# A transformer batch loop on one core: a deferred finish started later on VectorE, and unread products added on TensorE

## What is computed

```python
x = x + LN(attn1(LN(x)))      # 16 heads of 16, rotary, causal, window of 250
s = LN(x)                     # the second source
y = attn2(s)                  # full attention, keys and values through a 64-wide projection
x2 = rmsnorm(s + y) * n1w
out = x2 + shared(x2) + sum over the two chosen of 8 experts of gate * (swiglu(x2 @ W1) @ W2[e])
x = x + LN(rmsnorm(out) * n2w)
```

## Time and profile before

| | us |
|---|---|
| median of 3 runs | 2101.24 (2096.93 to 2102.88) |
| profiled execution, its own time | 2093.5 |
| its span, first to last instruction | 2091.7 |
| PE busy, DVE busy, ACT busy, POOL busy | 1893.1, 1370.5, 828.7, 381.4 |

### The profile page before, as it was taken

One profiled execution on the slowest core, in us unless ns is written; L12 is line 12 of the kernel. 1 busy time (PEld: TensorE's weight loads), 2 busy tenths in 40 slices (PEclk: granted clock), 3 DMA queues, 4 the chain that ended last, 5 costly groups with the idle time before them and its releaser, 6 DMA issues.

```text
span 2091.7 us, 28659 instructions
## 1 busy us (share of the span) xinstructions
PE 1893.1 (91%) x9484; PEld 1082.9 (52%) x9484; DVE 1370.5 (66%) x4293; ACT 828.7 (40%) x1730; POOL 381.4 (18%) x675
## 2 busy tenths in 40 slices
PE   6868898999999998999989999999989999899886
PEld 4343455636455464644646455553646546464565
DVE  6457464775858576585866857586675858668264
ACT  3534434254333534335442453326343353534310
POOL 1346013101221013200241012210122002410000
PEclk8676879999999997999999999899989999899898
DMA  2027102200141100401032010321014110220312
GB/s 84 2 81 277 46 32 92 101 25 28 42 152 42 42 31 27 177 12 52 22 112 101 2 51 32 122 80 42 11 42 152 42 49 24 100 103 2 131 51 100
DMA packets 33314, 141.95 MB, mean 68 GB/s; under 512 B 4368, under 2 KB 15248, under 8 KB 28560
## 3 DMA queue, kind: packets, MB, share of 16 engines
q1 hardware_dynamic: 29840, 121.27, 16.0%
q0 software_dynamic: 3328, 18.88, 2.4%
HBM read 118.11 MB, written 20.97 MB: 66 GB/s over the span
## 4 chain that ended last, share of the span: by engine, by line
PE 63%; DVE 27%; issue 6%; ACT 3%; POOL 0%; DMA 0%; SPq 0%; DVEq 0%; ACTq 0%; POOLq 0%
PE fb L820 12%; PE ot L767 11%; PE fb L797 8%; PE sm L725 8%; DVE negmax L1118 6%; PE st L753 4%; PE st L693 3%; DVE acc L1311 2%; DVE sm L1115 2%; PE st L709 2%; PE dn L693 2%; PE fb L816 2%; PE sm L753 2%; DVE stats L1032 2%; PE dn L735 1%
## 5 line engine op out<-in xcount | busy, mean ns | idle before, releaser
L611 ACT ACTIVATE probs<-st 128x512 f32<-128x512 f32 (+3 forms) x832 | 397.9, 507 | 452.9 <-PE st L753 450.1
L820 PE MATMUL fb<-w_r,h_r 128*128 128x512 f32 x1536 | 434.1, 415 | 0.0
L725 PE MATMUL sm<-k_t,q_t 48*128 48x512 f32 (+3 forms) x864 | 321.2, 457 | 65.1 <-DVE negmax L1115 39.0
L753 PE MATMUL st<-q_t,k_t 64*128 64x512 f32 (+3 forms) x832 | 307.4, 464 | 16.7 <-ACT probs L611 16.5
L820 PEld LDWEIGHTS fb<-w_r,h_r 128*128 128x128 f32 x1536 | 268.5, 189 | 103.7 <-issue 57.5
L1118 DVE TENSOR_REDUCE negmax<-sm 128x1 f32<-128x512 f32 x416 | 270.7, 685 | 78.2 <-PE sm L725 77.8
L725 PEld LDWEIGHTS sm<-k_t,q_t 48*128 48x128 f32 x864 | 146.6, 197 | 298.6 <-DVE negmax L1115 117.4
L1115 DVE CUSTOM_DVE_ANT_0 sm<-sm,mask_qk 128x384 f32<-128x384 f32 (+1 forms) x448 | 204.3, 465 | 111.9 <-PE sm L725 110.3
L797 PE MATMUL fb<-stack,wup_r 128*128 128x512 f32 x768 | 267.3, 468 | 3.2 <-DVE sg L1289 3.1
L767 PE MATMUL ot<-probs,v_s 128*32 128x512 f32 (+3 forms) x2048 | 266.0, 549 | 2.3 <-POOL probs L477 2.3
L436 POOL TENSOR_TENSOR stack<-rot,stack 128x256 fp32r<-128x256 f32 x64 | 50.0, 781 | 1000.2 <-ACT stack L547 1000.2
(11 more groups left out here) (173 smaller groups left out, 2511.0 us busy)
## 6 DMA issues: line engine op xcount, KB each, us to landing
w_r<-w_parts SPq DMA_DIRECT2D x32, 2048.0 KB, 7.9
wup_r<-wup_parts SPq DMA_DIRECT2D x64, 512.0 KB, 4.4
w_parts<-w_r POOLq DMA_DIRECT2D x4, 2048.0 KB, 9.3
x_s<-in_L_attn_query SPq DMA_DIRECT2D x8, 512.0 KB, 4.8
q_t<-rot_b SPq DMA_DIRECT2D x256, 4.0 KB
wup_parts<-h_r POOLq DMA_DIRECT2D x2, 2048.0 KB, 8.2
x_kept<-o_s SPq DMA_DIRECT2D x8, 512.0 KB, 3.0
h_s<-in_L_ffn_W_experts POOLq DMA_DIRECT2D x8, 512.0 KB, 5.7
```

The source lines that it names most:

```text
L611: nc.scalar.activation(probs[:, n % PSLOTS, 0:hi - lo], score_bank(m)[:, 0:hi - lo], ACT.Exp, scale=float(D) ** -0.5).then_inc(s_ex, 1)
L725: mm(max_bank(w, a)[:, 0:hi - lo], q_t[r:r + MROW, b, t * P:(t + 1) * P], k_t[r:r + MROW, b, lo:hi], start=True, stop=True).then_inc(s_sm, 1)
L753: mm(score_bank(w)[:, 0:hi - lo], k_t[r:r + SK, b, j * P:(j + 1) * P], q_t[r:r + SK, b, lo:hi], start=True, stop=True).then_inc(s_st, 1)
L820: last = mm(fb[q % 2][:, :], h_r[:, h, m, rows], w2_r[:, k % 2, w, m, :], start=(m == 0 and n == 0), stop=(m == NH - 1 and n == 2))
```

## The change

`unread(bank, n)` issues n products of the identity with a piece of the output weights into a bank; nobody reads them. In batch 1, which has no e, they stand where later batches multiply e's last sets: 6 behind the transposes of xa, 4 after tile 2 and 4 after the last stacks in `heads`, and 2 in each of the first four units of the attention. In batches 1 to 7, 2 more stand in the middle stage between the transposes of xn and the wait for their copies. On DVE the generators are taken apart: `gates(f)` is stepped as before, and `finish(e)` begins at m = 30, with two steps to a unit.

```diff
--- before.py
+++ after.py
@@ -67,6 +67,7 @@
 SOURCE_FIRST, SOURCE_STEPS = 18, 2
 STEPS_AT_LAST = 9
 SOURCE_FROM = 36
+FINISH_FROM, FINISH_STEPS = 30, 2
 
 
 LEAD_WIDE, TAIL_WIDE = (range(2 * GH, LEAD - GH), range(0, LEAD - GH)), ALL - LEAD + 4
@@ -840,6 +841,11 @@
                 if t == NT - 1:
                     last.then_inc(s_gl, 1)
 
+            def unread(bank, n):
+
+                for _ in range(n):
+                    mm(bank[:, 0:E], ident[:, :], wout_t[:, 0, :], start=True, stop=True)
+
             def in_pairs(w, wide):
 
                 return (() if w % 2 else (w, w + 1)) if wide else (w,)
@@ -849,8 +855,11 @@
                     if f is not None and a == 0:
                         if m == ROWS_FROM:
                             experts_rows(f, i)
-                        if e is not None and m in LAST_OUT_AT:
-                            expert_out(e, OUT_LEAD, LAST_OUT_AT.index(m))
+                        if m in LAST_OUT_AT:
+                            if e is not None:
+                                expert_out(e, OUT_LEAD, LAST_OUT_AT.index(m))
+                            else:
+                                unread(fb[1], 2)
                     if a == 0 and m == LAST_STACKS_AT:
                         if f is not None:
                             pe.wait_ge(s_xh, (f + 1) * N_XH)
@@ -907,12 +916,14 @@
                         last = project_rows(st[m][:, (t % 2) * E:(t % 2 + 1) * E], w, xn_t, t)
                     last.then_inc(s_pj, 1)
 
-            def heads(i, a, f):
+            def heads(i, a, f, second=False):
 
                 def beside(t):
                     if f is not None:
                         for q, m in OUT_HEADS[a][t]:
                             expert_out(f, q, m)
+                    elif second and a == 0:
+                        unread(fb[0], 2 * len(OUT_HEADS[a][t]))
 
                 for t in range(NT):
                     if t >= 2:
@@ -946,10 +957,12 @@
                 transpose_rows(xa, pair, s_tp)
                 if e is not None:
                     out_rows(e, OUT_ROWS)
+                elif f is not None:
+                    unread(fb[1], 6)
                 pe.wait_ge(s_tc, i * N_TC + NC)
                 if f is not None:
                     pe.wait_ge(s_pr, i * N_PR)
-                heads(i, 0, e)
+                heads(i, 0, e, f is not None)
                 if f is None:
                     pe.wait_ge(s_w, 16 * N_LOADS)
                 attention(i, f, e, 0)
@@ -957,12 +970,11 @@
                 if f is not None:
                     for q in OUT_FIRST:
                         out_rows(f, q)
-
-                    for _ in range(2):
-                        mm(dn[:, 0:E], ident[:, :], wout_t[:, 0, :], start=True, stop=True)
-
+                    unread(dn, 2)
                 pe.wait_ge(s_xn, i + 1)
                 transpose_rows(xn, pair, s_tp)
+                if f is not None:
+                    unread(st[1], 2)
                 pe.wait_ge(s_tc, i * N_TC + 3 * NC)
                 for c in range(NC):
                     last = mm(st[0][:, :], wc_s[:, c, :], xn_t[:, c, :], start=(c == 0), stop=(c == NC - 1))
@@ -1159,15 +1171,13 @@
                 beside(NT)
 
             def attention(i, f, e, a, more):
-                def beside():
-                    if f is not None and a == 0:
-                        yield from gates(f)
-                    if e is not None and a == 0:
-                        yield from finish(e)
-                    if a == 1 and more:
-                        yield from first_source(i + 1)
-
-                others, begin = beside(), (GATES_FROM, SOURCE_FROM)[a]
+                none = iter(())
+                if a == 0:
+                    others = gates(f) if f is not None else none
+                    later = finish(e) if e is not None else none
+                else:
+                    others, later = first_source(i + 1) if more else none, none
+                begin = (GATES_FROM, SOURCE_FROM)[a]
                 for m in range(-LEAD, ALL):
                     if a == 0 and m == LAST_STACKS_AT:
                         copy_stacks(i, a, NT - 1)
@@ -1191,7 +1201,13 @@
                                 expert_out(f, q)
                     if m >= begin:
                         next(others, None)
+                    if a == 0 and m == FINISH_FROM:
+                        run(others)
+                    if a == 0 and m >= FINISH_FROM:
+                        for _ in range(FINISH_STEPS):
+                            next(later, None)
                 run(others)
+                run(later)
                 normalise(i, a, NGR - 1)
                 out_now(f, sorted({q for part in OUT_END[a] for q, m in part}))
```

## The result

| | before | changed |
|---|---|---|
| median, us (6 runs each) | 2100.47 | 2109.04 (2103.36 to 2115.69) |
| ratio | | 1.0048 [1.003, 1.0066] |
| profiled execution, own time / span | 2093.5 / 2091.7 | 2103.36 / 2101.5 |
| mean granted clock | 0.926 | 0.924 |

A forecast was written before the change was run, and what follows sets the result against it. The prediction took TensorE (busy 91%) as the bound, losing time waiting for DVE and running at 1.2 GHz after such waits. Its terms, -6.7 - 5.7 + 2 = -10.4 us, took 2101.2 to 2090.8 us, range 2072 to 2108.

The forecast's parts named there:

- Part one: Batch 1's first stage: unread products keep the clock up, 50.8 us against 57.46, a gain of 6.7 us.
- Part two: Middle stage, batches 1 to 7: two products stop four clock falls, 6.4 us gained less 0.7 delay: 5.7 us.
- Part three: First attentions of batches 2 to 7: moved finish delays unit 38, 0.3 us more in each, 2 us lost.
- I leave batches 3 and 6 their extra falls: Part three's assumption that the first attentions of batches 3 and 6 (63.1 and 60.8 us) keep their additional clock falls.
- Rival (d): Units 16 to 22 of first attentions: four more batches fall like batch 3, +8 us, 2109 us; chance 0.16.
- (a): First attentions: the clock holds behind the last maxima too, -37 us, 2064 us; chance 0.10.
- (b): Middle stage: the two products do not hold the clock, -4 us, 2097 us; chance 0.14.
- (c): Batch 1's first stage: the clock falls despite the products, -2 us, 2099 us; chance 0.13.

The follow-up runs named there:

- e1: Kernel before plus all unread products of the change, finish stepped as before; 2106.11 us, ratio 1.0044.
- e12: Changed kernel with no finish step at units 35 to 37, three unread products at unit 38 and one at unit 22; 2081.50 us, ratio 0.9909.
- e14: Changed kernel with six unread products in the middle stage instead of two; 2105.05 us, ratio 1.0027.
- e3: Kernel before plus batch 1's unread products only; 2095.77 us, ratio 0.9989.
- e4: Kernel before plus only the two unread products in the middle stage of batches 1 to 7; 2117.03 us, ratio 1.0085.
- e6: e3 plus four unread products at unit 38 of each first attention from batch 1 on; 2089.68 us, ratio 0.9957.
- e11: e10 plus three unread products at unit 38, before the last maxima's transposes; 2092.60 us, ratio 0.9981.
- e2: Kernel before with only the finish moved and doubled, no new products; 2102.86 us, ratio 1.0028.
- e8: e2 with no finish step at units 35 to 37; 2074.74 us, ratio 0.9924.
- e10: Changed kernel without the middle-stage products and with no finish step at units 35 to 37; 2082.72 us, ratio 0.9902.
- e7: e6 plus two unread products before the transposes at unit 22; 2077.71 us, ratio 0.9897.

## Why the prediction was wrong

*Part one* was right in the stage (51.1 us, forecast 50.8), and its risk was real: of ten profiled executions with these products three (e1, e12, e14) fell in the stage and took 56.7 or 56.8. The gain of 6.7 us did not reach the end: e3 is 0.9989 [0.997, 1.0008].

*Part two* is the step that failed: "Gain 6.4 us, less 0.7: 5.7 us". The stage moved as forecast (26.2 us seven times, no delay). The sum took it that 1.6 us cut from a stage is 1.6 us cut from the end and that all other stages keep their times. By itself the edit costs 17 us (e4), in first attentions of 63 to 64 us and second ones of 84.3. In the changed kernel's profile the two parts gave their 12.8 us, and 15.0 came back in batch 1's first attention and in second attentions, for which the sum has no term. The falls of the middle stage weren't a property of it either: they went away in e6 and e11 by edits in another stage.

*Part three* was near. Forecast were 28.3 us up to unit 30 (28.2), PE passing unit 38 at 38.5 to 39.4 us (1566.55 - 1528.3 = 38.3), a wait of 3.5 to 4.5 us there (3.41), a fall behind it (it came), and 57.8 to 58.7 us in all: 58.7 and 59.0 where nothing fell in front. Its size was some 0.5 us low a batch, and two errors partly cancel in it: unit 38 was passed at 38.3 us, just before the range, while from there to unit 44 it took 8.45 us for the 7.8 of the sum (1575 - 1566.55), and the rest 12.0 for 11.5. Alone the part costs 2.7 us by the medians and 2.5 in the six first attentions of the profile (358.2 against 355.7), for the 2 forecast. The fall itself has two courses: in e2's profile it came with the wait at unit 38 in batches 2 and 3, but in batches 5 to 7 some 30 us into the stage, before that wait, for 13.7 us, at nearly the same length (58.5 or 58.6). What I had not seen is how much could be had by keeping these steps away from unit 38: 22 to 26 us (e2 against e8), some of it in other stages.

*"I leave batches 3 and 6 their extra falls"* is the same mistake as in part two: the falls were taken as properties of the batches. Batch 3's fall in front is in batches 2 to 5 of the changed kernel, and batch 6's (from 5 us on) in none.

*Rival (d)* had the number, 2109 us, and the kind of mechanism: "a shift of the batches can make others fall". Batches 2 to 5 fell in front and took 60.1 to 63.3 us. But that its number came out is luck: it has 18.8 us in first attentions of batches 2 to 7, where the profile has 8.5, and 2.5 came in e2 from part three alone. It lacked batch 1's first attention (4.2 us) and the second attentions (10.8), nearly half of what was given back, where I had seen no fall and so looked for no wait; and it got a chance of 0.16 where the trace had six batches with the same instructions and four different lengths. *(a)* and *(b)* did not happen; *(c)* did not in the changed kernel's profile, but did in those of e1, e12 and e14.

The Trainium skill's sentence on transposes ("TensorE: Matmul & The Clock Gate", Part 4: PE-mode transpose), by which two products might not do, was not borne out as an obstacle: with them no middle stage fell in any of the eight profiles that have them. Nor do the runs show that the products are needed, as e6 and e11 had none.

**What stays open.** Shown is that the same instructions take 57.8 or 63 to 64 us, that the middle products by themselves lengthen stages which they don't touch, and that the time does not follow the work added (0, 2, 4, 6 products). Not shown is that the moved starts do it, which is the likeliest reading, nor a rule that says from the times which batch will fall. The medians of e8 to e10 rest on runs that scatter by 25 to 40 us.

## What to carry to other kernels

Where the clock of TensorE falls in some repetitions of a stage and not in others, the lengths of the stages can't be added: before an edit of 1 or 2 us is counted, take the waits of PE in *all* stages as places at which the next fall can land (here the clock fell behind a wait of 0.87 us in the changed kernel and held behind one of 0.88 in the kernel before). Then try to shorten the waits that every repetition has, by taking work out from between the producer and the wait (e8) or by filling them (e7), rather than only the short stretch in which the clock happened to be low. Even that is no rule: filling unit 38 gained in e6 (four products, 0.9957), and in e11 (three) it lost most of what the pause had gained (0.9981, e10 without it 0.9902). And time each part of such a change by itself: here one part gained nothing that can be told, one cost 17 us and one could be turned from a ratio of 1.0028 into one of 0.9924 by leaving three units out. And time each kernel many times, as one profile shows one of several courses (e8 had two, some 20 us apart).

## What the runs showed of the hardware

In second attentions of 84.3 us TensorE's clock was low for 20.5 us at a stretch, for 7.8 us lost; in the middle stage 3.4 us low cost 1.6; in batch 1's first attention 13.7 us low cost 4.2. Eight records of unread float32 products (128x256) are listed with 1.99 us in e7, where the prediction's price gives 1.86 and some 0.1 for the listing. Beside a GpSimd subtraction of 128x512 (1.26 us) a DVE instruction on two SBUF operands took 1.1 to 1.2 us instead of some 0.2: before, a step of the finish (1.11 us), after, the split of the maxima (1.20).
